# The kept rows folded down to one column per sample by accumulating DMAs, and weighed directly

## The reference

```
prev = x0 = inputs                                # (2048, 39, 16)
for W, b in ((W0, b0), (W1, b1), (W2, b2)):       # 128 filters each
    z = relu(einsum('bhk,bmk,hmf->bfk', prev, x0, W.reshape(h, 39, 128)) + b)
    results.append(z[:, :64])                     # the kept rows
    prev = z[:, 64:]                              # the state, goes on to the next layer
pooled = sum over k of concatenate(results)       # (2048, 192)
return pooled @ W_lin                             # (2048, 1)
```

## Time and profile before

| | |
|---|---|
| median of the runs | 1971.02 us |
| the profiled execution | 1970.57 us |
| its span (first to last instruction) | 1968.6 us |
| TensorE busy | 1962.8 us (100%) |
| VectorE busy | 1912.1 us (97%) |
| ScalarE busy | 586.7 us (30%) |
| GpSimd busy | 154.5 us (8%) |
| DMA queue of SyncE (q1) | 303.05 MB, 71.2% of 16 engines |
| DMA queue of GpSimd (q0) | 23.87 MB, 7.8% of 16 engines |

### The profile page before, as it was taken

How to read it: one execution, slowest core, us unless ns; L and a number is a source line. 1 busy time by engine, 2 the same in 40 slices (tenths; PEclk the granted TensorE clock), 3 DMA queues, 4 the chain that set the end, 5 groups by cost and what they waited for, 6 DMA issues and landing times.

```text
span 1968.6 us, 29931 instructions
## 1 busy us (share of the span) xinstructions
PE 1962.8 (100%) x10304; PEld 739.1 (38%) x10304; DVE 1912.1 (97%) x1445; ACT 586.7 (30%) x717; POOL 154.5 (8%) x186
## 2 busy tenths in 40 slices
PE   9999999999999999999999999999999999999999
PEld 3333343333333333333343333333333333333333
DVE  8989999999999999999999999999999999999988
ACT  2333223332133322333222332223332133322332
POOL 1001000010100100001000010010100100000000
DMA  7999988788977889778798777987778977789720
GB/s 179 189 194 186 188 174 169 162 171 175 191 165 158 175 167 199 168 154 175 159 207 169 154 173 162 195 183 157 168 159 183 192 160 166 164 175 197 149 43 1
DMA packets 122523, 327.45 MB, mean 166 GB/s; under 512 B 24529, under 2 KB 43370, under 8 KB 122501
## 3 DMA queue, kind: packets, MB, share of 16 engines
q1 hardware_dynamic: 97539, 303.05, 71.2%
q0 software_dynamic: 24192, 23.87, 7.8%
q10 hardware_dynamic: 770, 0.23, 0.1%
HBM read 303.11 MB, written 0.01 MB: 154 GB/s over the span
## 4 chain that ended last, share of the span: by engine, by line
PE 97%; DVE 2%; DMA 0%; issue 0%; ACT 0%; ACTq 0%; DVEq 0%
PE acc L845 37%; PE acc L722 23%; PE acc L921 20%; PE acc L850 11%; PE acc L910 2%; PE acc L714 2%; DVE prod L408 1%; PE acc L789 1%; PE acc L935 1%; PE acc L928 1%; DMA bias<-b 0%; DVE prod L414 0%; PE acc L729 0%; ACT prev L1043 0%; ACTq L1141 0%
## 5 line engine op out<-in xcount | busy, mean ns | idle before, releaser
L408 DVE TENSOR_TENSOR prod<-prev,x_bc 128x2048 f32<-128x2048 f32 x511 | 1139.7, 2283 | 11.1 <-PE acc L722 9.4
L845 PE MATMUL acc<-prod,w_sb 128*64 128x512 f32 x3360 | 748.4, 593 | 0.0
L921 PE MATMUL acc<-prod,w_sb 128*64 128x512 f32 x1064 | 462.4, 593 | 0.1
L845 PEld LDWEIGHTS acc<-prod,w_sb 128*64 128x64 f32 x3360 | 237.3, 137 | 442.4 <-issue 391.4
L928 PE MATMUL acc<-prod,w_sb 128*64 128x512 f32 x840 | 384.3, 593 | 0.0
L722 PE MATMUL acc<-x_rot,w_sb 128*64 128x512 f32 x1240 | 277.5, 593 | 0.0
L1090 ACT ACTIVATE diff<-acc 64x256 f32<-64x256 f32 x56 | 21.3, 380 | 735.3 <-PE acc L850 735.0
L921 PEld LDWEIGHTS acc<-prod,w_sb 128*64 128x64 f32 x1064 | 143.9, 137 | 248.3 <-issue 193.5
L414 DVE TENSOR_TENSOR prod<-prev,x_bc 128x1024 f32<-128x1024 f32 x193 | 230.0, 1218 | 1.5
L381 DVE TENSOR_TENSOR x_rot<-x_rot,x_rep 128x1024 f32<-128x1024 f32 (+1 forms) x186 | 214.5, 1222 | 1.3 <-issue 0.3
L1014 ACT ACTIVATE prev<-acc,bias 32x1024 f32<-32x1024 f32 x140 | 155.1, 1108 | 3.1 <-DVE prod L408 0.9
(11 more groups left out here) (100 smaller groups left out, 1246.7 us busy)
## 6 DMA issues: line engine op xcount, KB each, us to landing
x_bc<-x SPq DMA_DIRECT2D x312, 256.0 KB, 15.5
x_bc<-x SPq DMA_DIRECT2D x156, 512.0 KB, 21.4
x_rot<-x SPq DMA_DIRECT2D x155, 312.0 KB
x_rot<-x SPq DMA_DIRECT2D x217, 156.0 KB
x_bc<-x SPq DMA_DIRECT2D x124, 128.0 KB, 11.0
x_rep<-x SPq DMA_DIRECT2D x62, 192.0 KB
x_bc<-x_bc POOLq DMA_DIRECT2D x56, 128.0 KB, 10.1
x_rot<-x SPq DMA_DIRECT2D x124, 44.0 KB
```

Of the source, the lines that this page charges most:

```text
L408: mul = nc.vector.tensor_tensor(prod[:, s:s + w, :], twice, x_bc[:, u, t:t + w, :], ALU.mult)
L845: mm = nc.tensor.matmul(acc1[f, h, :], w[:, f], prod[:, s, BANK * h:BANK * h + BANK], start=False, stop=stop, skip_group_check=closed)
L921: nc.tensor.matmul(acc2[0:HALF, u, :], w, prod[:, s, 0:BANK], start=(pos == 1), stop=False)
```

## The change

`fold` now takes the number of halvings: four for `res01` (1024 to 64 columns) and three for `res2` (512 to 64), each issued when the one before has landed. In the loop the two channel sums become `weigh_folded01` and `weigh_folded2`, which wait for the last fold and weigh the 64 columns where they lie, without a TENSOR_REDUCE; the weighing of `res2` moves behind the layer-0 products and behind the weighing of `res01`. ScalarE waits for `pooled01` and `pooled2`, that is for the weighing, where it waited for the sum. The blocks outside the loop still sum with a TENSOR_REDUCE, with constant semaphore values.

```diff
+    FOLDS01, FOLDS2 = (NB // BB).bit_length() - 1, (BANK // BB).bit_length() - 1
...
+            def weigh_folded01(i, a, folded):
+
+                dve.wait_ge(folded01, folded)
+                nc.vector.tensor_scalar(pool[:, bass.ds(i * BB, BB)], res01[a][:, 0:BB], wl_col[:, 0:1], None,
+                                        ALU.mult).then_inc(pooled01, 1)
+
+            def weigh_folded2(i, folded):
+
+                dve.wait_ge(folded2, folded)
+                dve.wait_ge(pooled01, i + 2)
+                column = pool[:, bass.ds(i * BB, BB)]
+                nc.vector.scalar_tensor_tensor(column, res2[:, 0:BB], wl_col[:, 1:2], column, ALU.mult,
+                                               ALU.add).then_inc(pooled2, 1)
...
-                    channel_sum2(i - 2, folded=i * 32 - 32)
                     products0(i + 1)
-                    channel_sum01(i - 1, 1 - u, folded=i * 32 - 32)
+                    weigh_folded01(i - 1, 1 - u, i * (16 * FOLDS01) - 16 * FOLDS01)
+                    weigh_folded2(i - 2, i * (16 * FOLDS2) - 16 * FOLDS2)
                     products2(i, u, i * (2 * CH) + CH)
...
-            def fold(res, n, folded, done):
-
-                pool.sem_inc(adds_asked, 1)
-                pool.dma_start(res[:, 0:n // 2], res[:, n // 2:n], accum_op=ALU.add).then_inc(folded, 16)
-                pool.wait_ge(folded, done + 16)
-                pool.sem_inc(adds_asked, 1)
-                pool.dma_start(res[:, 0:n // 4], res[:, n // 4:n // 2], accum_op=ALU.add).then_inc(folded, 16)
+            def fold(res, n, times, folded, done):
+
+                for m in range(times):
+                    n //= 2
+                    if m > 0:
+                        pool.wait_ge(folded, done + 16 * m)
+                    pool.sem_inc(adds_asked, 1)
+                    pool.dma_start(res[:, 0:n], res[:, n:2 * n], accum_op=ALU.add).then_inc(folded, 16)
...
                     pool.wait_ge(res01_ready, i * 2 + 1)
-                    fold(res01[1 - u], NB, folded01, i * 32 - 64)
+                    fold(res01[1 - u], NB, FOLDS01, folded01, i * (16 * FOLDS01) - 32 * FOLDS01)
                     pool.wait_ge(res2_ready, i + 1)
-                    fold(res2, BANK, folded2, i * 32 - 64)
+                    fold(res2, BANK, FOLDS2, folded2, i * (16 * FOLDS2) - 32 * FOLDS2)
...
             def evacuate0(i, a):
                 act.wait_ge(acc0_full, i + 1)
                 spread(prev[0], acc0[:, a, :, :], 0)
-                act.wait_ge(sum01_ready, i + 1)
+                act.wait_ge(pooled01, i)
                 keep01(acc0[:, a, :, :], 0, a)
...
             def evacuate2(i, u, full):
                 act.wait_ge(acc2_full, full)
-                act.wait_ge(sum2_ready, i + 1)
+                act.wait_ge(pooled2, i + 1)
```

More of the change, by code:

```diff
@@ L535, in channel_sum, with channel_sum01 @@
             def channel_sum(total, res):
-                return nc.vector.tensor_reduce(total[:], res.rearrange("p (k b) -> p b k", b=BB),
+                return nc.vector.tensor_reduce(total[:], res[:].rearrange("p (k b) -> p b k", b=BB),
                                                mybir.AxisListType.X, ALU.add)
[L540 to L545, removed]
+            def channel_sum01(i, a, n):
+                dve.wait_ge(res01_ready, i * 2 + 3)
@@ L546, in channel_sum01 @@
                 dve.wait_ge(pooled01, i + 1)
-                channel_sum(sum01, res01[a][:, 0:NB if folded is None else QTR]).then_inc(sum01_ready, 1)
-                dve.wait_ge(sum01_ready, i + 3)
+                channel_sum(sum01, res01[a]).then_inc(sum01_ready, 1)
+                dve.wait_ge(sum01_ready, n)
                 nc.vector.tensor_scalar(pool[:, bass.ds(i * BB, BB)], sum01[:], wl_col[:, 0:1], None,
                                         ALU.mult).then_inc(pooled01, 1)
[L552 to L557, removed]
+            def weigh_folded01(i, a, folded):
+                dve.wait_ge(folded01, folded)
+                nc.vector.tensor_scalar(pool[:, bass.ds(i * BB, BB)], res01[a][:, 0:BB], wl_col[:, 0:1], None,
+                                        ALU.mult).then_inc(pooled01, 1)
@@ L558, in channel_sum2 @@
+            def weigh_folded2(i, folded):
[4 more added lines that the diff above has]
+                                               ALU.add).then_inc(pooled2, 1)
+            def channel_sum2(i, n):
+                dve.wait_ge(res2_ready, i + 3)
                 dve.wait_ge(pooled2, i + 1)
-                channel_sum(sum2, res2[:, 0:BANK if folded is None else P]).then_inc(sum2_ready, 1)
@@ L560, in channel_sum2 @@
-                dve.wait_ge(sum2_ready, i + 2)
+                channel_sum(sum2, res2).then_inc(sum2_ready, 1)
+                dve.wait_ge(sum2_ready, n)
                 dve.wait_ge(pooled01, i + 2)
@@ L567, in _ @@
             nc.vector.memset(res2[:], 0.0).then_inc(res2_cleared, 1)
-            dve.sem_inc(sum01_ready, 2)
-            dve.sem_inc(sum2_ready, 1)
             dve.sem_inc(pooled01, 1)
@@ L606, in _ @@
             nc.vector.tensor_scalar(wl1_all[:], ones[:], wl_col[:, 0:1], None, ALU.mult).then_inc(wl2_ready, 1)
-            channel_sum01(0, 0)
+            channel_sum01(0, 0, 1)
             products2(1, 1, 3 * CH)
@@ L622, in _ @@
             products1(LAST - 1, 0, STEPS - 1, n)
-            channel_sum2(LAST - 3)
+            channel_sum2(LAST - 3, 1)
             products0(LAST)
-            channel_sum01(LAST - 2, 1)
+            channel_sum01(LAST - 2, 1, 2)
             products2(LAST - 1, 0, n + CH, range(TAIL_RUNS))
             products1_last(LAST, 1, STEPS, n + CH + TAIL)
-            channel_sum2(LAST - 2)
-            channel_sum01(LAST - 1, 0)
+            channel_sum2(LAST - 2, 2)
+            channel_sum01(LAST - 1, 0, 3)
             products2(LAST - 1, 0, n + 2 * CH, range(TAIL_RUNS, NR), phase=2 * CH)
             products2(LAST, 1, n + 3 * CH, range(NR + 1), last=True, phase=3 * CH)
-            channel_sum2(LAST - 1)
+            channel_sum2(LAST - 1, 3)
             dve.wait_ge(res01_ready, LAST * 2 + 3)
-            channel_sum(sum01, res01[1][:]).then_inc(sum01_ready, 1)
+            channel_sum(sum01, res01[1]).then_inc(sum01_ready, 1)
             dve.wait_ge(last_ready, 1)
@@ L995, in _ @@
                 nc.tensor.matmul(acc_last, wl2_all[:], res2[:, BB * k:BB * k + BB], start=(k == 0), stop=False)
-            pe.wait_ge(sum01_ready, 2 + NBLK)
+            pe.wait_ge(sum01_ready, 4)
             nc.tensor.matmul(acc_last, wl1_all[:], sum01[:], start=False, stop=True).then_inc(last_ready, 1)
@@ L1046, in evacuate0_first @@
                 act.wait_ge(acc0_full, 1)
-                act.wait_ge(sum01_ready, 1)
                 for h in range(NH):
@@ L1168, in _ @@
             act.wait_ge(chunk_used, n + 4 * CH + RING)
-            act.wait_ge(sum2_ready, LAST + 1)
+            act.wait_ge(pooled2, LAST + 1)
             nc.scalar.activation(res2[:], acc2[:, 1, :], ACT.Relu, bias=bias[:, 2:3]).then_inc(res2_ready, 1)
```

## The result

The changed kernel takes 1974.26 us in the median of 20 runs (1971.12 to 1977.34), the kernel before 1971.03 us in the median of 20; the ratio is 1.0016, 95% interval [1.0009, 1.0023]. Of the kernel before, 19 runs took 1969.78 to 1972.30 us and one, which the ratio leaves out, 3483 us. The change makes the kernel slower by 3.2 us: the interval is clear of 1, but the step is smaller than the 3.9 us that the prediction took as the least that can be told from no change. The profiled execution took 1976.4 us, with a span of 1974.6 us.

A forecast was written before the change was run, and what follows sets the result against it. TensorE was taken to bound the kernel. 1970.57 us + 6.4 for the first-pass wait - 0.5 for lighter VectorE work = 1976.5, forecast as 1976.9 us for the median; own range 1975.5 to 1979, 8 in 10 within 1970 to 1986.

The forecast's parts named there:

- TensorE sets the pace: Steady pass: TensorE is busy 121.50 of 121.5 us, so work taken from VectorE gives back about 0.5 us in all.
- VectorE has no slack at the end of layer 2: End of layer 2: VectorE arrives level with TensorE, so delay of its layer-2 products beyond what the change frees is paid in full.
- First pass: wait 7 us, cost 6.4 us: First loop pass: third res2 fold lands about 191.2 us, asked for at about 183.7; layer-2 products start 6.4 us later, paid once.
- lower bound of 5.0: First-pass cost in us if each fold step is 0.4 us faster and the last res2 fold lands at 189.8 us.
- 0.05 us a pass from VectorE's lighter load: Last chunks of layer 2: TensorE waits less for VectorE, 0.05 us or less in each of 14 passes, about 0.5 in all.
- The cushion of 1.3 us: Each block: with the reductions gone VectorE would start layer-2 products about 1.3 us earlier, so a shorter wait is free.
- Steady even block: fold at 1033.8 to 1034.4, asked for at 1034.1; odd block 969 to 973.5 against 973.7: Last res2 fold's landing against VectorE's question in steady passes: even block waits 0 to 1.5 us, odd block none; cost 0.
- Rival A: Steady even blocks: third res2 fold also lands past the cushion; 1979 to 1998 us, most likely near 1984; chance 0.20.
- Rival B: First pass: last fold lands before 184.8 us, five landings of 8 us or less, so no wait; 1970.5 us; chance 0.17.
- Rival C: Layer-2 weight loads: TensorE's waits for VectorE's products are real stalls, 5 to 10 us come back; 1961 to 1966 us; chance 0.05.

The follow-up runs named there:

- moved_only: The kernel before with only its channel sum of res2 moved behind the layer-0 products and the sum of res01; 1968.81 us, ratio 0.999.
- weigh_early: The changed kernel with the weighing of res2 back ahead of the layer-0 products, where its channel sum was; 2056.96 us in two runs.

## Why the prediction was right, and where it was off

The side, the mechanism and the range of 8 in 10 (1970 to 1986 us) held. The range of the forecast itself, 1975.5 to 1979 us, did not: the median of 1974.26 lies 1.2 us under it, and by the 3.9 us that the prediction asked for it would count as no change, to which the prediction gave 0.23 and not 0.72. Only the narrower interval of 20 runs calls it slower. Point by point:

- *TensorE sets the pace, VectorE has no slack at the end of layer 2.* Right; the 7.70 us reach the end whole. TensorE's gap is spread over layer 2 as forecast, 5.0 us of the pass idle and the rest in stretched matmuls. VectorE's 22.5 us of saved work bought 1.6 us, and the move alone buys as much.
- *First pass: wait 7 us, cost 6.4 us.* The chain was built right, step for step (issues forecast at 151.4, 165.2, 166.1, 177.3 and 188.1, seen at 151.69, 165.69, 166.29, 179.10 and 188.94). The first res2 fold took 12.2 us where I took 10.3, and the cost came to 7.7. For the profiled execution I had 1976.5 us and it took 1976.4: that is luck, since the wait cost 1.3 us more than I had and the passes gave back 1.1 us more. The median of the runs is lower: 1974.26 = 1971.0 - 1.6 + 4.9, so by this sum, which no trace shows, the wait typically costs 4.9 us, under the lower bound of 5.0 that I gave. This term was mis-sized: I took it from the landings of one execution and gave no room to their scatter. The two profiled executions of the changed kernel (1976.40 and 1976.19 us) lie near the top of their runs, so waits of 9.2 and 9.1 us are not typical either.
- *0.05 us a pass from VectorE's lighter load.* Mis-sized: 0.12 us. The stretched matmul is 0.05 of it. I missed that TensorE also loses time a little later, in layer 1 of the odd block: the 14 matmuls of line 845 at 1061.24 take 3.34 us in the kernel before and 3.26 us in `moved_only` (at 1060.59). And I gave the gain to the work removed when the moved line is enough.
- *The cushion of 1.3 us.* This step failed. "VectorE would start the layer-2 products about 1.3 us earlier" is wrong: they start 9.01 instead of 9.28 us behind the mix, 0.27 us earlier, and the other 1.0 us is a wait for ScalarE's state rows. The conclusion (a fold up to a microsecond late is free) stood by that wait, not by my cushion: here I was lucky. I had not asked what is late next.
- *Steady even block: fold at 1033.8 to 1034.4, asked for at 1034.1; odd block 969 to 973.5 against 973.7.* Right: in the even blocks the fold was late five more times, by 0.4 us at the most; in the odd blocks never. Rival A did not happen; the longest of these waits was well inside 1.0 us. `weigh_early` shows how near it was: asking 6.9 us earlier costs 83 us.
- *Rival B* needed 8 us per landing; the five took 11.0, 13.3, 12.2, 9.2 and 3.4 us, 49 us together instead of 40. The Trainium skill's page "DMA: Bandwidth & Descriptors", section "Anatomy of one DMA — SWDGE (gpsimd) path", puts one DMA of this queue at about 2.0 us plus its bytes over 436 GB/s, which is 2.3 us for 128 KB (an estimate from that page). The trace comes near it only while the loads are quiet (2.7 us for 128 KB in the median); beside the loads it has 11.7 us. *Rival C*: TensorE's weight-load waits were no stalls; no run has passes under 121.37 us, 0.12 us less than before.

## What to carry to other kernels

A chain of dependent small DMAs costs its number of landings, and beside the loads of this kernel each landing in the first pass took 9 to 14 us; put independent chains in turn, and ask for the result as late as possible. Work out the first pass of a loop by itself: here the same chain landed level with the question in the steady passes and 9 us late in the first. Taking work from an engine that isn't the bound buys at most the stalls it causes, and a moved line may buy the same: `moved_only`, the old kernel with one line moved, beats both (1968.81 us), and no run with more folds is measurably faster than it.

## What the runs showed of the hardware

When SyncE's loads run, the landing time of an accumulating DMA shows next to no dependence on its size between 32 and 128 KB. Issues of the changed kernel by size, count, KB, median us to landing:

```profile
res<-res POOLq DMA_DIRECT2D x42, 128.0 KB, 11.7
...
res<-res POOLq DMA_DIRECT2D x42, 64.0 KB, 10.2
...
x_seed<-x_seed POOLq DMA_DIRECT2D x14, 128.0 KB, 2.7
res<-res POOLq DMA_DIRECT2D x42, 32.0 KB, 10.2
...
x_seed<-x_seed POOLq DMA_DIRECT2D x14, 64.0 KB, 5.5
```

The 128 KB of x_seed at 2.7 us go out when the loads are quiet, the 64 KB at 5.5 us when they have just begun again (992.23 us in the steady pass shown, first load at 990.02).

Most of this time goes by before the fold's first packet. The res2 fold of 128 KB issued at 1008.55 us took 12.1 us. From 1008.6 to 1016.5 us only packets of SyncE's queue (q1) ran, 438 of them; the 144 of GpSimd's (q0) lie in the 4.5 us behind. The queues of the two stretches (packets, MB, share of 16 engines), the only one of the first and the second one of the second:

```profile
q1 hardware_dynamic: 438, 1.37, 103.2%
```

```profile
q0 software_dynamic: 144, 0.13, 18.4%
```

For the x_seed fold of 256 KB issued at 984.89 us, in a quiet stretch, the first packet follows 1.4 us behind the issue, and it lands in 3.3 us. VectorE was at work on products for 7.83 of the 7.90 us beside the slow fold and for all of the 3.90 us from 984.9 beside the quick one, so its work does not tell them apart. What holds the packets back was not tested.

After the 2.5 us stop in the first pass TensorE was slowed: the granted clock was 0.50 from 197.5 to 200.8 us, that is the lower of its two levels (2.4 and 1.2 GHz), and 1.00 again from 200.9. It had been at work in 1.49 of the 4 us from 192. This cost nothing here, since VectorE held the pace until 215 us.

```profile
192.00:196.00 4.00, 1.49 (x8) 0.20 (x4) 3.54 (x4) 3.35 (x4) 2.65 (x3) 1.00 0.58 136
197.50:200.80 3.30, 3.30 (x12) 1.42 (x10) 3.30 (x2) 3.26 (x4) 0.00 (x0) 0.50 1.02 241
```
